# The low half of the turned exponentials, moved from VectorE to GpSimd by way of an SBUF copy

## What is computed

```python
q_big = apply_rope(einsum('bshk,hkq->bshq', hidden_q @ Wq.T, w_kc_q))
q_r = einsum('bshq,hqr->bhsr', q_big, W_qr)
k_r = einsum('bld,hdr->bhlr', kv_r, W_kr)
attn = softmax(einsum('bhsr,bhlr->bhsl', q_r, k_r))
ctx_c = einsum('bhsl,bld->bhsd', attn, kv_r)
ctx_lat = einsum('bhsd,hkd->bhsk', ctx_c, w_kc_kv)
return ctx @ Wo.T
```

## Time and profile before

| what | value |
|---|---|
| median of three runs | 611.46 us (610.19 to 612.35) |
| the profiled execution, its own time | 612.25 us |
| its span, first to last instruction | 610.4 us |
| mean granted TensorE clock | 0.879 of full |
| busy: TensorE, VectorE, ScalarE, GpSimd | 458.7, 431.1, 262.3, 236.2 us |
| attention steps n = 0 to 63 | 201 to 443 us of the span |

### The profile page before, as it was taken

One profiled execution on the slowest core, in us unless ns is written; L12 is line 12 of the kernel. 1 busy time (PEld: TensorE's weight loads), 2 busy tenths in 40 slices (PEclk: granted clock), 3 DMA queues, 4 the chain that ended last, 5 costly groups with the idle time before them and its releaser, 6 DMA issues.

```text
span 610.4 us, 11625 instructions
## 1 busy us (share of the span) xinstructions
PE 458.7 (75%) x4466; PEld 346.7 (57%) x4466; DVE 431.1 (71%) x960; ACT 262.3 (43%) x588; POOL 236.2 (39%) x240
## 2 busy tenths in 40 slices
PE   1884626766367799899879997799741899999991
PEld 0564502434255577678657775677631477777781
DVE  3248985899855587788868977887733388878870
ACT  0444432544331545545525543455510365556630
POOL 1057760111103123333223421542032347777875
PEclk9996866878558899999969997999785699999997
DMA  7891092000051000000000410100001346676624
GB/s 209 276 338 21 6 362 103 0 2 0 1 184 58 2 1 2 2 2 2 1 25 14 124 51 2 37 20 2 5 31 38 84 162 182 183 183 183 161 23 44
DMA packets 37687, 47.69 MB, mean 78 GB/s; under 512 B 7424, under 2 KB 32768, under 8 KB 37440
## 3 DMA queue, kind: packets, MB, share of 16 engines
q1 hardware_dynamic: 29552, 40.97, 20.8%
q0 software_dynamic: 4224, 4.79, 5.0%
q10 hardware_dynamic: 3856, 1.18, 0.9%
HBM read 41.10 MB, written 8.55 MB: 81 GB/s over the span
## 4 chain that ended last, share of the span: by engine, by line
PE 48%; DVE 28%; ACT 6%; issue 5%; DMA 5%; POOL 5%; ACTq 3%; POOLq 0%; SPq 0%; DVEq 0%; another core or an unknown queue 0%
PE psum L1292 9%; PE psum L1501 7%; PE psum L1352 5%; PE psum L1514 4%; PE psum L1337 3%; PE psum L1319 3%; PE psum L1366 3%; PE psum L1312 3%; DMA se<-in_w 3%; PE psum L1392 3%; ACT lw L634 2%; DVE se L957 2%; ACT lw L607 2%; DVE am L855 2%; DVE lw L845 2%
## 5 line engine op out<-in xcount | busy, mean ns | idle before, releaser
L455 POOL TENSOR_TENSOR lw<-lw 128x512 f32<-128x512 f32 x48 | 60.7, 1269 | 135.6 <-DVE lw L913 135.4
L641 ACT ACTIVATE lw<-psum 128x512 f16<-128x512 f32 x64 | 38.2, 597 | 84.5 <-PE psum L1352 84.3
L1292 PE MATMUL psum<-lp 128*128 128x256 f16 x576 | 70.2, 277 | 5.5 <-DVE scat L1026 3.7
L634 ACT ACTIVATE lw<-psum,nmax 128x256 f32<-128x256 f32 x128 | 59.2, 471 | 11.7 <-DVE nmax L924 11.7
L1292 PEld LDWEIGHTS psum<-lp 128*128 128x128 f16 x576 | 54.8, 99 | 14.2 <-DVE scat L1026 3.9
L514 POOL TENSOR_TENSOR lw<-lw 128x320 f16<-128x320 f32 x64 | 47.9, 749 | 36.1 <-DVE lw L1099 32.7
L1501 PE MATMUL psum<-lw,se 128*128 128x320 f16 x384 | 56.6, 307 | 1.0 <-issue 0.7
L929 DVE TENSOR_TENSOR lw<-psum,lw 128x512 f16<-128x512 f32 x64 | 43.8, 684 | 15.7 <-ACT lw L641 14.6
L702 ACT ACTIVATE lw<-psum,b1w 128x320 f16<-128x320 f32 x64 | 33.7, 527 | 46.8 <-PE psum L1501 46.8
L1099 DVE TENSOR_SCALAR lw<-psum,b1w 128x320 f32<-128x320 f32 x64 | 35.3, 551 | 20.3 <-ACT lw L702 19.7
L1352 PE MATMUL psum<-identf,lw 128*128 128x128 f32 x256 | 43.7, 296 | 7.5 <-DVE lw L929 4.0
(11 more groups left out here) (201 smaller groups left out, 1022.1 us busy)
## 6 DMA issues: line engine op xcount, KB each, us to landing
se<-in_w SPq DMA_DIRECT2D x16, 1024.0 KB
dispatch<-in_empty SPq DMA_DIRECT2D x4, 662.5 KB, 9.6
lw<-dispatch SPq DMA_DIRECT2D x8, 265.0 KB
lp<-in_Wq SPq DMA_DIRECT2D x1, 2048.0 KB, 14.2
se<-in_WoT SPq DMA_DIRECT2D x1, 2048.0 KB, 16.6
lp<-in_w_kc_q SPq DMA_DIRECT2D x1, 1536.0 KB, 18.5
x_sb<-in_x SPq DMA_DIRECT2D x2, 512.0 KB, 6.0
se<-in_gate_wT SPq DMA_DIRECT2D x1, 1024.0 KB, 9.5
```

The lines of the kernel that those rows point to most:

```text
L455: nc.gpsimd.tensor_tensor(rope[:, c % QT, :], t1[:, c % 2, :], t2[:, c % 2, :], ALU.add)\
L634: A_(e_sb[:, n % 2, st * S:(st + 1) * S], bank[3 + n % 2][:, st * S:(st + 1) * S], ACT.Exp, bias=nmax[:, n % 2, st:st + 1], accum_out=esum ...
L1292: ins = M(tile_bank(c)[:, half * S:(half + 1) * S], m1[w][:, kc, half, col:col + P], (yth, ytl)[a][:, kc, b * S:(b + 1) * S], start=(n == ...
```

## The change

In each step ScalarE first copies bank 5 as float32 to `raw` in SBUF and signals `a_tf`, waits for that itself, and makes the float16 high half from the copy. The low half is made by GpSimd from `raw` and the high half. TensorE's next turn waits for `a_tf` instead of the low half, context waits for GpSimd's signal `g_at` instead of VectorE's. On GpSimd at_low(n) stands ahead of the rotations and the routing of step n. ScalarE's copy also waits until GpSimd has read the buffer two steps back. VectorE's at_low is gone.

```diff
@@ gpsimd
             for c in range(2 * QT):
                 rotate(c)
+            def at_low(n):
+
+                pool.wait_ge(a_at, n + 1)
+                if n >= 2:
+                    pool.wait_ge(p_cx, n - 1)
+                nc.gpsimd.tensor_tensor(at[1][:, n % 2, :], raw[:, n % 2, :], at[0][:, n % 2, :], ALU.subtract)\
+                    .then_inc(g_at, 1)
+
             for n in range(NHB):
+                at_low(n)
                 for c in tiles_at(n):
                     rotate(c)
@@ scalar
             def at_high(n):
                 act.wait_ge(p_at, n + 1)
+                if n == 0:
+                    act.wait_ge(v_krl, 3)
                 if n >= 2:
+                    act.wait_ge(g_at, n - 1)
                     act.wait_ge(p_cx, n - 1)
-                A_(at[0][:, n % 2, :], bank[5][:, :], ACT.Copy).then_inc(a_at, 1)
+                A_(raw[:, n % 2, :], bank[5][:, :], ACT.Copy).then_inc(a_tf, 1)
+                act.wait_ge(a_tf, n + 1)
+                A_(at[0][:, n % 2, :], raw[:, n % 2, :], ACT.Copy).then_inc(a_at, 1)
@@ vector
-            def at_low(n):
-                dve.wait_ge(a_at, n + 1)
-                V.tensor_tensor(at[1][:, n % 2, :], bank[5][:, :], at[0][:, n % 2, :], ALU.subtract).then_inc(v_at, 1)
...
-                at_low(n)
@@ tensor, turn_scores(n)
                 if n >= 1:
-                    pe.wait_ge(v_at, n)
+                    pe.wait_ge(a_tf, n)
@@ tensor, context(n)
-                pe.wait_ge(v_at, n + 1)
+                pe.wait_ge(g_at, n + 1)
```

More of the change, by code:

```diff
@@ L267, in program @@
         p_qz, a_qz, v_qz = sem("p_qz"), sem("a_qz"), sem("v_qz")
-        p_sc, v_max, a_exp, p_at, a_at, v_at, p_cx = (sem("p_sc"), sem("v_max"), sem("a_exp"), sem("p_at"),
-                                                     sem("a_at"), sem("v_at"), sem("p_cx"))
+        p_sc, v_max, a_exp, p_at, a_tf, a_at, g_at, p_cx = (sem("p_sc"), sem("v_max"), sem("a_exp"), sem("p_at"),
+                                                     sem("a_tf"), sem("a_at"), sem("g_at"), sem("p_cx"))
         v_norm, p_ct, a_ct, v_ct, p_out = sem("v_norm"), sem("p_ct"), sem("a_ct"), sem("v_ct"), sem("p_out")
```

## The result

The changed kernel takes 644.01 us, the median of four runs (642.08 to 648.96), against 611.87 us before on the same chip: a ratio of 1.0543 [1.0479, 1.0606]. The prediction was 625.0 us with a range of 617 to 636; the sign is right, the size lies outside. The profiled execution took 642.08 us, its span is 639.8.

What follows compares the result with a forecast made beforehand. A serial circle of turn, copy, exponentials, scores was taken to bound the loop. Terms 7.3 + 2.0 + 1.9 - 1.6 + 4.0 = +13.6 us on the median 611.46 gave 625 us, range 617 to 636.

Steps and rivals of the forecast that it cites:

- Direction and bound: Attention loop: a serial circle of turn, copy, exponentials, scores bounds it; VectorE's lost subtractions gain nothing in plain groups; slower 0.89.
- ScalarE's term: Second copy in series: +0.91 us in each of eight plain groups (7.3), 2.0 us for n = 0, 24, 40.
- x: Time the second ScalarE copy adds to the circle in each step: 0.67 us, bounds 0.49 and 0.80.
- GpSimd's subtraction: Low half on GpSimd: 1.00 us each, bounds 1.00 and 3.2, hidden in plain groups behind TensorE's next scores and turn.
- n = 36 term: At n = 36, after GpSimd writes the tokens' rows, context(37) comes 1.9 us late instead of 0.9: +1.9 (0.9 to 3).
- n = 28 to 31 and 44 to 47: Low half waits behind four GpSimd DMAs, but VectorE's lists are relieved: -0.9 and -0.7, together -1.6; +3.0 if the clock falls.
- rival B: Shared port: GpSimd's subtraction and VectorE's small two-input products and weight-part subtractions exclude each other; 8 us, total 633; chance 0.10.
- n = 56 to 63: Loop's end: about 1.9 at the turn of n = 60, given back before the slots; the DMAs then cost +4.0 (2 to 5.5).
- the sign of C: What would show the clock rival: a granted clock under 1.00 from 216 to 301 us.
- rival C: Clock: longer TensorE idling brings three more low stretches of some 7 us, half of each lost; +10, total 636; chance 0.07.
- A: The forecast as summed, with its own range of 619 to 631 us; chance 0.72.
- list term: The -1.6 us for n = 28 to 31 and 44 to 47, where VectorE's routing lists no longer have the low half behind them.

Runs made afterwards that it cites:

- filler_h0: The changed kernel plus ten idle matmuls on TensorE at h = 0, where it waits for the exponentials; 630.24 us, ratio 1.0319.
- before_filler: Control: the kernel before the change plus only ten idle matmuls on TensorE at h = 0; 605.24 us, ratio 0.9929.
- lists_all_filler: The kernel before with GpSimd making the low half only at n = 28, 44, 60, sixteen idle matmuls there, ten at other h = 0 steps; 605.21 us.
- vector_long_filler: The changed kernel with the low half back on VectorE, twenty idle matmuls at n = 12, 28, 44, ten at other h = 0 steps; 621.69 us.
- low_on_vector: The changed kernel with the low half given back to VectorE, ScalarE's two copies left as changed; 633.35 us, ratio 1.0344.

## Why the prediction was wrong, step by step

**Direction and bound: right.** The circle of turn, copy, exponentials, scores bounds the plain groups, and moving VectorE's work to GpSimd gained nothing there.

**ScalarE's term: right.** x is 0.67 as said, the second copy 0.632 us (said 0.62). At full clock on both sides (filler_h0 less before) the eight plain groups grew by 7.9 us (said 7.3: a plain group grew by 0.99 and not 0.91, of it 0.32 at h = 2 where 0.24 was counted), the three others (n = 0, 24, 40) by 2.5 (said 2.0).

**GpSimd's subtraction: mis-sized, without effect where it was hidden.** It took 1.157 us where "1.00 us each" was taken from the earlier trace rows. In plain groups it is hidden as said. The n = 36 term was +1.6 (said +1.9).

**n = 28 to 31 and 44 to 47: wrong.** The step "Without at_low(28) ahead, the turn gains 1.42 us; latent then runs at full clock, and VectorE reaches the slots earlier" gave -1.6. Measured: +3.3 and +3.9, of which 2.5 and 1.7 go with the idle matmuls. The half about GpSimd's DMAs held (3.27 and 3.09 us of waiting, foreseen about 3). The half about the relief fell: the low clock did not go (0.81 and 0.80), and with idle matmuls in both kernels (filler_h0 against before_filler) the two groups are 4.5 us and 4.4 us longer, a part of that still clock (0.93 against 1.00). What the relief is worth at full clock is the 0.3 us of lists_all_filler: the turn's 1.42 us go, and the next wait on VectorE, for `norm` behind the same list, takes their place; the walk left it out. A further loss can be read in VectorE's timeline of the changed kernel: its list meets GpSimd's subtraction.

```profile
308.82 1.12 DVE L994 TENSOR_TENSOR gates<-el,es 128x16 f32<-128x16 f32 x1
...
310.66 0.76 DVE L1002 CAST idf<-i 128x4 f32<-128x4 uint32 x1
```

```profile
310.24 1.16 POOL L488 TENSOR_TENSOR lw<-lw 128x512 f16<-128x512 f32 x1 [0.33 <-ACT lw L655]
```

and in the kernel before

```profile
304.24 0.17 DVE L992 CAST idf<-i 128x4 f32<-128x4 uint32 x1
```

The cast starts while GpSimd subtracts (310.24 to 311.40) and ends with it. That is rival B's mechanism, about 0.6 us here, and a further 0.8 where VectorE's normalising at L734 meets it (400/409/1250 ns, minimum, median, maximum of 24). In the whole kernel these casts, the list's copies (L1018, up to 1.14 us instead of 0.17), the last instruction of the places (L1036, up to 1.13 instead of 0.23) and the normalising became 5.1 us longer, in VectorE's busy time. How much of that anybody waited for no run shows; the 8 us of B in full do not fit, since all of GpSimd's place is 8.5 us at most and TensorE's waits behind the DMAs come to 9.0 by themselves.

**n = 56 to 63: nearly right.** Said +4.0 (2 to 5.5) with 1.9 at the turn of n = 60; measured at full clock +1.85 at that turn. From there to the last projection the changed kernel is 4.0 us longer than before (3.6 with idle matmuls), which makes +5.4 to +5.9, at the upper end. The DMAs' cost was as foreseen; of the 2.4 us that the low halves' leaving was to give back (1.9 and 0.5) the traces show 0.9: the first DMA starts 8.27 us after the turn of n = 60 (465.46 less 457.19) where it was 9.21 (440.76 less 431.55).

**The clock: the step that failed.** The prediction summed its terms at an unchanged clock and gave the dips a chance of 0.07 only as an alternative, with the words "It kept 2.4 GHz over 216 to 301 us with 1.25 us gaps". That row shows that the clock held with 1.25 us, not that it holds with 1.91; the same text had computed 1.9. What it had named as the sign of C, a granted clock under 1.00 from 216 to 301 us, is there: 0.96 in the changed kernel's plain groups. The price of rival C came out near (+10; measured 13.8 on the medians, 12.0 between turn 0 and turn 60), in part by luck: it was three stretches of some 3.5 us, and there were five groups of about 1.5 each and 4.2 us at n = 28 and 44. Its place was wrong: C did not take A's place but came on top of it. 625 plus 10 is 635. With the added dips filled the kernel stands 630.2 - 610.6 = 19.7 us over the one before as it is, against 13.6 said, the difference being mostly the two list groups (+4.6 over the term). In short, the term that was put at nothing, the clock, measured 12 to 14 us, and the list term of -1.6 measured +3.0 even with idle matmuls; the two make nearly all of the miss of 18.5 (32.1 us on the medians, 13.6 said).

The range's lower end has an error of sum: the lower bounds add up to +7.2 (4.4, 1.5, 0.9, -1.6 and 2.0), not +6; the upper ones to +23 as said.

In all: the circle 11.1 us, GpSimd's place 8.5, the clock 13.8, each from the medians of a pair of kernels: vector_long_filler against before, filler_h0 against it, changed against filler_h0. That they add up to the whole 33.4 us is no test, since each pair begins where the one ahead ends. The first is low for the work itself, as the kernel before has two dips of its own (5.9 us at n = 28 and 44, from before_filler) which vector_long_filler has in smaller form; against before_filler it is 16.5. So the split between work and clock depends on whose dips one counts: with idle matmuls in both, the change costs 630.2 - 605.2 = 25 us.

The Trainium skill, TensorE: Matmul & The Clock Gate, section A second HAM failure mode, says that short idles between groups of matmuls, coming often enough, make the clock swing. The trace of before did not show it, those after agree: 0.96 and, in low_on_vector, 0.92 over the plain groups with a wait of 1.91 us in each, 1.00 with 1.74. No run here shows that it is this and not the idling's sum that counts. The rule of two SBUF inputs that the prediction cites does not cover the cast and the normalising, which read one. Another one does: the Trainium skill, SBUF — State Buffer, section Who interferes with whom, lists copy, cast and tensor_scalar among those that can take the pair of ports shared with GpSimd. The trace agrees with 0.76 us for a 128x4 cast beside GpSimd.

## What to carry to other kernels

When a change lengthens an idle time of TensorE that recurs, add the clock to the sum as a term, not as an unlikely rival: a level that was held with the old gaps says nothing about longer ones. Before moving work to an engine that looks idle, list what already stands in its queue ahead of the new place (here four DMAs, 5 us), and who waits behind. When two kernels are compared to price a part, first look whether their clocks dip in the same groups; if not, fill TensorE's idle time in both and compare again, and read the granted clock of the groups, as the length of single matmuls can miss a low stretch.

## What the runs showed of the hardware that was not expected

- With one wait of 1.74 us in a group of 14.84 us the granted clock was 1.00 over the plain groups; with one of 1.91 us in a group of 15.20 it was 0.96 in one kernel and 0.92 in another, and the dips were not in the same groups. One execution of each was traced. A dip in a plain group cost 1.35 to 1.56 us and in most reached over one turn.
- Ten matmuls with an unused result, put into the idle time, cost nothing (15.20 us a plain group with and without) and gave back 13.8 us to the changed kernel and 0.7% [0.45%, 0.98%] to the one before. They did not hold the clock over TensorE's wait of 3.27 us behind the DMAs (0.93 over that group).
- A 128x512 copy on ScalarE takes nearly the same from SBUF to float16 (0.632 us) as from PSUM to float32 (0.598). What differed was the start: 0.49 us after the one ahead when both read the bank, 0.63 when it waited for the first one's own signal.
- On GpSimd the same subtraction took 1.157 us in the loop, with little spread (1.148 to 1.190), beside 1.00 in the setup; 1.7 times VectorE's 0.684.
- VectorE's small instructions grow when they meet GpSimd's subtraction: a 128x4 cast from 0.17 to 0.76 us, a 128x2 copy from 0.17 to 1.14, a 128x4 tensor_scalar from 0.23 to 1.13.
